# The x tiles of an attention and FP4 feed-forward layer loaded one by one, and the order of work on four engines written anew

## What is computed

```python
xn = layernorm(x)
q, k = l2norm(xn @ Wq.T), l2norm(xn @ Wk.T)      # 16 heads of 16
v = xn @ Wv.T
attn = softmax(q @ k.T + alibi, keys in a window of 128)   # ahead of and at the query
s = (attn @ v) @ Wo.T
h = silu(fq(xn) @ fq(w_gate).T) * (fq(xn) @ fq(w_up).T)    # 256 -> 704
g = silu(fq(h) @ fq(w_down).T)                             # 704 -> 256
out = x + s * g
# fq: FP4 (E2M1) rounding in blocks of 16 with a scale from the block's largest value
```

## Time and profile before

| | |
|---|---|
| median of three runs | 531.66 us (530.77 to 533.08) |
| the profiled execution | 533.7 us, of it a span of 532.0 us from the first to the last instruction |
| PE busy | 481.7 us, 91% |
| DVE, ACT, POOL busy | 427.3, 401.6, 428.6 us (80%, 75%, 81%) |
| mean granted TensorE clock | 0.962 |
| DMA | 29.36 MB, mean 55 GB/s |

### The profile page before, as it was taken

One profiled execution on the slowest core, in us unless ns is written; L12 is line 12 of the kernel. 1 busy time (PEld: TensorE's weight loads), 2 busy tenths in 40 slices (PEclk: granted clock), 3 DMA queues, 4 the chain that ended last, 5 costly groups with the idle time before them and its releaser, 6 DMA issues.

```text
span 532.0 us, 13894 instructions
## 1 busy us (share of the span) xinstructions
PE 481.7 (91%) x4962; PEld 410.7 (77%) x4962; DVE 427.3 (80%) x848; ACT 401.6 (75%) x572; POOL 428.6 (81%) x941
## 2 busy tenths in 40 slices
...
GB/s 308 59 40 41 40 41 42 41 52 52 51 90 51 52 51 76 28 51 41 51 90 52 52 51 89 52 22 41 51 41 52 51 51 51 51 51 51 14 10 31
DMA packets 78037, 29.36 MB, mean 55 GB/s; under 512 B 67472, under 2 KB 77456, under 8 KB 77968
## 3 DMA queue, kind: packets, MB, share of 16 engines
...
...
## 4 chain that ended last, share of the span: by engine, by line
PE 71%; DMA 8%; DVE 7%; POOL 6%; issue 5%; ACT 2%; POOLq 0%; ACTq 0%; DVEq 0%
PE up L277 12%; PE bank_b L468 11%; PE gt L430 11%; PE gt L277 9%; DMA qk_slots<-qk_stack 7%; PE bank_q L277 7%; PE scores L392 6%; PE gt L283 6%; PE bank_b L283 4%; PE bank_b L277 3%; PE gt L445 3%; DVE h_amax L602 1%; DVE qk_stack L661 1%; DVE hT_lo L641 1%; DMA keyfac<-key_factors 1%
## 5 line engine op out<-in xcount | busy, mean ns | idle before, releaser
L966 ACT ACTIVATE probs<-scores 128x1024 f32<-128x1024 f32 (+1 forms) x128 | 128.6, 1005 | 1.6 <-PE scores L392 0.8
L1101 POOL TENSOR_SCALAR_AFFINE_SELECT probs<-probs 128x512 f32<-128x512 f32 x128 | 82.5, 647 | 5.2 <-ACT probs L966 2.8
L1108 POOL TENSOR_SCALAR_AFFINE_SELECT probs<-probs 128x512 f32<-128x512 f32 x120 | 75.1, 638 | 2.0
L1134 POOL TENSOR_TENSOR h_q<-h_grid,h_scale 128x704 f32<-128x704 bf16 x32 | 44.4, 1388 | 38.2 <-DVE h_grid L624 38.2
L974 ACT ACTIVATE gate<-gt 128x704 f32<-128x704 f32 x32 | 24.3, 758 | 54.5 <-PE gt L277 54.5
L430 PE MATMUL gt<-wdn_hi,hT_hi 128*128 128x256 f32 x192 | 61.0, 318 | 0.6 <-DVE hT_lo L632 0.6
L468 PE MATMUL bank_b<-probs,vals 128*32 128x128 f32 x1984 | 60.8, 274 | 0.7 <-DVE att L686 0.7
L468 PEld LDWEIGHTS bank_b<-probs,vals 128*32 128x32 f32 x1984 | 52.2, 110 | 7.3 <-issue 7.2
L430 PE MATMUL gt<-wdn_lo,hT_hi 128*128 128x256 f32 x192 | 54.9, 286 | 0.0
L430 PE MATMUL gt<-wdn_hi,hT_lo 128*128 128x256 f32 x192 | 54.8, 285 | 0.0
L392 PE MATMUL scores<-qk_slots 48*128 48x256 f16 x480 | 47.2, 275 | 6.7 <-DMA qk_slots<-qk_stack 3.7
...
## 6 DMA issues: line engine op xcount, KB each, us to landing
...
qk_slots<-qk_stack SPq DMA_TRANSPOSE x32, 3.7
...
```

Source lines behind the costliest of these rows:

```text
L966: e.activation(probs[j % P_BUFS][:, grp, :, side(j), :], sc[:, :, :, side(j), :].rearrange("p b e h q -> p (b e) h q"), ACT.Exp).then_inc( ...
L1101: e.affine_select(out=own, in_=own, compare_op=ALU.is_ge, fill=0.0, base=0, pattern=[[0, GRP], [-1, P]], channel_multiplier=1).then_inc(s_ ...
L1108: e.affine_select(out=part, in_=part, compare_op=ALU.is_gt, fill=0.0, base=0, pattern=[[0, GRP], [1, P]], channel_multiplier=-1).then_inc( ...
L1134: e.tensor_tensor(blocks(h_q[t % 2][:, 0:FF]), blocks(h_grid[:]), per_block(h_scale[:]), ALU.mult).then_inc(s_q_h, 1)
```

## The change

Three things are altered. The last 16 tiles of x are no longer loaded in groups of four behind a store; each is loaded alone (128 KB) by a new `refill(t - 5)`, which SP issues right behind the transpose of tile t, for t from 5 to 20. It waits for `add_x` of the tile whose slot it fills. Second, on PE, DVE, ACT and POOL the first three turns and what follows the last full turn are written out call by call, in an order of their own. Third, the order within the repeated turn is new: on PE only the last two pieces change places (`wo_mm` before the end of `down_mm`), and on DVE, ACT and POOL several steps move. Two waits are added on PE: `up_mm` waits for `lo_x` (and the first for all rounded gate and up weights), `tr_tail` waits for `q_h`. What each function computes stays as it was.

The diff, with the indentation cut by twelve columns and the removed lines of the old loops left out:

```diff
@@ -37,7 +37,6 @@
 X_GROUP = 4
 X_RING = 16
 P_BUFS, Q_SLOTS, S_BUFS, V_SLOTS, Y_BUFS, FG_BUFS, XN_BUFS = 3, 3, 2, 4, 3, 2, 4
-X_LOADS = TILES // X_GROUP
 GRP = 4
 LAST = TILES - 1
@@ -157,7 +156,8 @@
 l_wproj, l_wg, l_wu, l_wd, l_wo, l_keyfac, l_ident, l_qkT = (
 sem(f"l_{n}") for n in ("wproj", "wg", "wu", "wd", "wo", "keyfac", "ident", "qkT"))
-l_x = [sem(f"l_x{i}") for i in range(X_LOADS)]
+l_x = [sem(f"l_x{i}") for i in range(X_RING // X_GROUP)]
+l_refill = [sem(f"l_refill{i}") for i in range(TILES - X_RING)]
 stored = [sem(f"stored{i}") for i in range(Y_BUFS)]
 s_lot = [sem(f"lot{i}") for i in range(len(GU_LOTS) + len(WD_LOTS))]
 s_scales = [sem(f"scales{i}") for i in range(WD_SCALES + 1)]
@@ -365,6 +365,9 @@
     product(gt_all[:, 512:512 + HALF], xT[t % 2], KT, wgu, HALF, FF).then_inc(s_gate_mm, 1)
 def up_mm(f):
+    if f == 0:
+        e.wait_ge(s_lo_wgu, len(WGU_GROUPS))
+    e.wait_ge(s_lo_x, f + LAG + 1)
     if f >= 1:
         e.wait_ge(s_hc, chain(f - 1, GRID))
     product(up_all[:, H0:512], xT[f % 2], KT, wgu, FF, FF + HALF)
@@ -403,6 +406,7 @@
 def tr_tail(g):
     if exists(g):
+        e.wait_ge(s_q_h, g + 1)
         e.wait_ge(s_pv_t, g + 1)
         e.wait_ge(s_pad_h, min(g + 1, 2))
         done = transposes(bank_b[:, 0:2 * P], [h_q[g % 2][:, k * P:(k + 1) * P] for k in range(4, FT)])
@@ -475,66 +479,93 @@
     transposes(bank_b, [pv_t[:, g, :] for g in range(4)]).then_inc(s_back, 1)
 tr_x(0)
-for t in range(END + 1):
-    f, g = t - LAG, t - LAG - 1
-    if exists(t - 2):
-        scores(t - 2, 3)
+qk_mm(0)
+v_mm(0)
+tr_x(1)
+qk_mm(1)
+tr_x(2)
+scores(0, 0)
+tr_wgu(0)
+v_mm(1)
+tr_wgu(1)
+scores(0, 1)
+tr_wgu(2)
+tr_wgu(3)
+tr_wgu(4)
+scores(0, 2)
+qk_mm(2)
+tr_wgu(5)
+v_mm(2)
+up_mm(0)
+gate_mm(0)
+up_mm_last(0)
+scores(0, 3)
+tr_x(3)
+tr_wd(0)
+tr_wd(1)
+scores(1, 0)
+tr_wd(2)
+scores(1, 1)
+scores(1, 2)
+scores(1, 3)
+for t in range(3, TILES):
+    qk_mm(t)
+    v_mm(t)
+    gate_mm(t - 2)
+    scores(t - 1, 0)
+    pv(t - 3)
+    tr_x(t + 1)
+    up_mm(t - 2)
+    tr_h(t - 3)
+    scores(t - 1, 1)
+    up_mm_last(t - 2)
+    tr_tail(t - 3)
+    scores(t - 1, 2)
+    down_mm(t - 3, 0, 4)
+    scores(t - 1, 3)
+    back(t - 3)
     if exists(t - 4):
...
+        wo_mm(t - 4)
+    down_mm(t - 3, 4, FT)
+gate_mm(TILES - 2)
+pv(TILES - 3)
+scores(TILES - 1, 0)
+up_mm(TILES - 2)
+up_mm_last(TILES - 2)
+tr_x(TILES + 1)
+tr_h(TILES - 3)
+scores(TILES - 1, 1)
+tr_tail(TILES - 3)
+scores(TILES - 1, 2)
+down_mm(TILES - 3, 0, 4)
+scores(TILES - 1, 3)
+down_mm(TILES - 3, 4, FT)
+back(TILES - 3)
+wo_mm(TILES - 4)
+up_mm(TILES - 1)
+gate_mm(TILES - 1)
+up_mm_last(TILES - 1)
+tr_h(TILES - 2)
+pv(TILES - 2)
+tr_tail(TILES - 2)
+down_mm(TILES - 2, 0, 4)
+back(TILES - 2)
+down_mm(TILES - 2, 4, FT)
+pv(TILES - 1)
+wo_mm(TILES - 3)
+tr_tail(TILES - 1)
+tr_h(TILES - 1)
+back(TILES - 1)
+wo_mm(TILES - 2)
+tr_tail(TILES)
+down_mm(TILES - 1, 0, 4)
+down_mm(TILES - 1, 4, FT)
+wo_mm(TILES - 1)
 def vector_program(e):
 def ln_stats(t):
-    e.wait_ge(l_x[t // X_GROUP], 16)
+    e.wait_ge(l_x[t // X_GROUP] if t < X_RING else l_refill[t - X_RING], 16)
     if t >= 1:
         e.wait_ge(s_moments, t)
     e.bn_stats(stats[:], x_all[:, t % X_RING, :]).then_inc(s_stats, 1)
@@ -766,103 +797,142 @@
 ln_moments(0)
 ln_stats(1)
 ln_moments(1)
-ln_stats(2)
 scales_w(0)
 amax_x(0)
 norm_w(0)
+ln_stats(2)
+lo_wproj(0)
+ln_moments(2)
+lo_wproj(1)
+lo_x(0)
 wide_x(0)
-lo_wproj(0)
-lo_x(0)
-lo_wproj(1)
 scales_w(1)
+squares(0)
+round_w(0)
+rscale_x(0)
+norm_x(0)
+lo_x(1)
+values(0)
+norm_w(2)
+ln_stats(3)
+up_x(0)
 scales_w(2)
...
+ln_moments(3)
+unit(0)
+amax_x(1)
+grid_x(0)
+wide_x(1)
+lo_qk(0)
+round_w(2)
+rscale_x(1)
+norm_w(4)
+squares(1)
+ln_stats(4)
+scales_w(WD_SCALES)
+round_w(4)
+norm_x(1)
+lo_wgu(0)
+norm_w(6)
+ln_moments(4)
+amax_x(2)
+lo_wgu(1)
+ln_stats(5)
+lo_wgu(2)
+unit(1)
+lo_wgu(3)
+up_x(1)
+lo_x(2)
+lo_qk(1)
+values(1)
+lo_wgu(4)
+grid_x(1)
+wide_x(2)
+lo_wgu(5)
+squares(2)
+values(2)
+rscale_x(2)
+round_w(6)
+hidden(0)
+norm_x(2)
+ln_moments(5)
+amax_h(0)
+lo_wd(0)
+lo_wo()
+up_x(2)
+lo_wd(1)
+unit(2)
+grid_x(2)
+lo_qk(2)
+lo_x(3)
+amax_x(3)
+wide_h(0)
+lo_wd(2)
+for t in range(3, TILES):
+    wide_x(t)
+    rscale_h(t - 3)
+    rscale_x(t)
+    norm_h(t - 3)
+    norm_x(t)
+    values(t)
+    up_h(t - 3)
+    grid_h(t - 3)
+    up_x(t)
+    if exists(t + 1):
+        amax_x(t + 1)
+    squares(t)
     if exists(t + 3):
         ln_stats(t + 3)
-    if exists(t + 1):
-        amax_x(t + 1)
-    if exists(t):
-        up_x(t)
-        grid_x(t)
+    lo_x(t + 1)
     if exists(t + 3):
         ln_moments(t + 3)
...
+    grid_x(t)
+    lo_h(t - 3)
+    hidden(t - 2)
+    unit(t)
+    lo_tail(t - 3)
+    amax_h(t - 2)
+    lo_qk(t)
+    denom(t - 3)
+    wide_h(t - 2)
+    if exists(t - 4):
+        gated(t - 4)
+    attend(t - 3)
+rscale_h(TILES - 3)
+norm_h(TILES - 3)
+up_h(TILES - 3)
+grid_h(TILES - 3)
+hidden(TILES - 2)
+lo_x(TILES + 1)
+amax_h(TILES - 2)
+lo_h(TILES - 3)
+wide_h(TILES - 2)
+rscale_h(TILES - 2)
+norm_h(TILES - 2)
+lo_tail(TILES - 3)
+up_h(TILES - 2)
+grid_h(TILES - 2)
+gated(TILES - 4)
+denom(TILES - 3)
+attend(TILES - 3)
+hidden(TILES - 1)
+amax_h(TILES - 1)
+wide_h(TILES - 1)
+lo_h(TILES - 2)
+rscale_h(TILES - 1)
+norm_h(TILES - 1)
+lo_tail(TILES - 2)
+up_h(TILES - 1)
+denom(TILES - 2)
+attend(TILES - 2)
+grid_h(TILES - 1)
+gated(TILES - 3)
+lo_tail(TILES - 1)
+lo_h(TILES - 1)
+denom(TILES - 1)
+attend(TILES - 1)
+gated(TILES - 2)
+lo_tail(TILES)
+gated(TILES - 1)
 def scalar_program(e):
@@ -989,71 +1059,94 @@
 e.dma_start(keyfac[:], keyfac_d).then_inc(l_keyfac, 16)
 hi_wproj(0)
 hi_wproj(1)
+square_w(0)
 hi_x(0)
-square_w(0)
 square(0)
+hi_x(1)
+hi_wo()
 square_w(1)
+square_x(0)
+hi_q(0)
+hi_k(0)
+square_w(2)
 square_w(3)
-square_w(2)
-hi_x(1)
-square_x(0)
+square(1)
 square_w(4)
+exp(0, 0)
 square_w(5)
 hi_wgu(0)
...
+exp(0, 1)
+hi_wgu(1)
+square_x(1)
+hi_wgu(2)
+hi_wgu(3)
+square_w(7)
+hi_q(1)
+hi_x(2)
+hi_k(1)
+exp(0, 2)
+square_w(6)
+hi_wgu(4)
+square(2)
+hi_wgu(5)
+silu(0)
+exp(0, 3)
+hi_wd(0)
+hi_x(3)
+hi_wd(1)
+exp(1, 0)
+square_x(2)
+exp(1, 1)
+hi_wd(2)
+hi_q(2)
+hi_k(2)
+exp(1, 2)
+exp(1, 3)
+square(3)
+square_h(0)
+square_x(3)
+silu(1)
+exp(2, 0)
+hi_x(4)
+keep_pv(0)
+hi_h(0)
+exp(2, 1)
+hi_tail(0)
+exp(2, 2)
+hi_q(3)
+hi_k(3)
+for t in range(3, TILES):
+    exp(t - 1, 3)
+    down_silu(t - 3)
+    square_h(t - 2)
     if exists(t + 1):
+        square_x(t + 1)
         square(t + 1)
...
+    silu(t - 1)
+    exp(t, 0)
+    hi_x(t + 2)
+    keep_pv(t - 2)
+    hi_h(t - 2)
+    exp(t, 1)
+    hi_tail(t - 2)
+    exp(t, 2)
     if exists(t + 1):
         hi_q(t + 1)
-    if t == 0:
-        hi_wgu(4)
-    if exists(t + 1):
         hi_k(t + 1)
-    if t == 1:
-        hi_wd(2)
-    if exists(t):
-        exp(t, 3)
+square_h(TILES - 2)
+exp(TILES - 1, 3)
+down_silu(TILES - 3)
+silu(TILES - 1)
+hi_h(TILES - 2)
+keep_pv(TILES - 2)
+hi_tail(TILES - 2)
+square_h(TILES - 1)
+down_silu(TILES - 2)
+keep_pv(TILES - 1)
+hi_tail(TILES - 1)
+hi_h(TILES - 1)
+hi_tail(TILES)
+down_silu(TILES - 1)
 def gpsimd_program(e):
@@ -1194,70 +1287,103 @@
     e.tensor_scalar(xn[t % XN_BUFS][:], x_all[:, t % X_RING, :], neg_mean[:], rsq[0][:, NS - 1:NS],
                     ALU.add, ALU.mult).then_inc(s_xn, 1)
-for i in range(S_BUFS):
-    pad_stack(i)
+pad_stack(0)
+pad_stack(1)
 pad_vals()
-for i in range(len(wdn)):
-    pad_wd(i)
-for slot in range(V_SLOTS):
-    ones(slot)
+pad_wd(0)
+pad_wd(1)
+ones(0)
 ln_parts(0)
 root(-2)
 x_norm(0)
 ln_parts(1)
 root(-1)
+norm_w(1)
+x_norm(1)
+norm_w(3)
+ln_parts(2)
+floor_ss(0)
 scale_x(0)
...
+ones(1)
+root(0)
+ones(2)
+round_w(1)
+q_x(0)
+x_norm(2)
+round_w(3)
+scale_x(1)
+ln_parts(3)
+floor_ss(1)
+norm_w(5)
+mask_own(0, 0)
+norm_w(7)
+root(1)
+ones(3)
+round_w(5)
+round_w(7)
+x_norm(3)
+q_x(1)
+floor_ss(2)
+ln_parts(4)
+root(2)
+mask_own(0, 1)
+scale_x(2)
+mask_own(0, 2)
+mask_own(0, 3)
+mask_own(1, 0)
+mask_prev(1, 0)
+mask_own(1, 1)
+mask_own(1, 2)
+mask_prev(1, 1)
+x_norm(4)
+q_x(2)
+mask_prev(1, 2)
+mask_own(1, 3)
+mask_prev(1, 3)
+ln_parts(5)
+scale_x(3)
+scale_h(0)
+pad_h(0)
+pad_h(1)
+for t in range(3, TILES):
+    q_h(t - 3)
+    floor_ss(t)
+    root(t)
+    mask_own(t - 1, 0)
+    mask_own(t - 1, 1)
+    mask_own(t - 1, 2)
     if exists(t + 2):
...
+        x_norm(t + 2)
+    mask_prev(t - 1, 0)
+    mask_prev(t - 1, 1)
+    mask_own(t - 1, 3)
+    mask_prev(t - 1, 2)
+    q_x(t)
+    if exists(t + 1):
+        scale_x(t + 1)
+    scale_h(t - 2)
+    mask_prev(t - 1, 3)
+    if exists(t - 4):
+        add_x(t - 4)
+    if exists(t + 3):
+        ln_parts(t + 3)
+q_h(TILES - 3)
+scale_h(TILES - 2)
+mask_own(TILES - 1, 0)
+mask_prev(TILES - 1, 0)
+mask_own(TILES - 1, 1)
+mask_own(TILES - 1, 2)
+mask_prev(TILES - 1, 1)
+mask_prev(TILES - 1, 2)
+mask_own(TILES - 1, 3)
+q_h(TILES - 2)
+mask_prev(TILES - 1, 3)
+scale_h(TILES - 1)
+q_h(TILES - 1)
+add_x(TILES - 4)
+add_x(TILES - 3)
+add_x(TILES - 2)
+add_x(TILES - 1)
 def sync_program(e):
@@ -1271,9 +1397,12 @@
```

(92 more changed lines are left out.)

134 lines of the change are left out of this document (removed).

## The result

| | before | after | ratio (95% interval) |
|---|---|---|---|
| median, first comparison | 531.21 us | 525.4 us | 0.9881 (0.9843 to 0.9918) |
| median, beside the first experiments | 531.65 us | 524.99 us | 0.9877 (0.985 to 0.9904) |
| range of the executions there | 529.4 to 532.9 | 524.0 to 525.5 | |

I read it with the cuts of the earlier trace rows: up to turn 4, turns 4 to 30, and the rest (stretch, length, PE, PEld, DVE, ACT, POOL, PEclk, DMA).

A forecast was written before the change was run, and what follows sets the result against it. PE was taken to bound turns 4 to 30 (busy 390.4 of 395.5 us), not start or end. Loop -1.3, start +1.7, end -4.7 sum to -4.3: 529.4 us for the profiled execution, 527.4 median; 8-in-10 range 520.5 to 534.5.

The forecast's parts named there:

- The repeated turn: Turns 4 to 30: PE's 14.48 us per turn stays the floor, and no result comes late in the new order.
- the first rival: Repeated turn: POOL ends root late, so every turn pays; at 0.3 us in 27 turns 535.5 us; chance 0.16.
- The late transposes: DMA transposes in the loop: seven stay late, each with an instruction packet; three to eleven possible, 0.7 us each.
- The term of the loop: Turns 4 to 30: 1.3 us gained, 0.3 in each of two windows and 0.1 in each of seven.
- The start: Up to qk_mm(3): 1.7 us lost, bounds 0.5 to 3.0, with qk_mm(3) at 65.2 instead of 63.48.
- (a): Start, DVE's queue up to the end of round_w(4): ends at 38.9 us, 1.4 earlier without blocked durations.
- (b): Start: tr_wgu(1) waits for round_w(4), at 38.9 instead of 31.91; lo_qk(1) ends at 47.7 instead of 45.87.
- (c): Start, from qk_mm(2) to the end of gate: gate ends at 55.6 us against 52.6, where silu starts.
- (d): Start, ACT's chain from silu to scores: 9.6 us and 0.3 of gaps, qk_mm(3) at 65.5.
- The end: Last long chain and final projections: 4.7 us gained, bounds 1.5 and 6.0.
- The clock: End: PE's clock stays full instead of 0.53 for 7.3 us, as PE's idle stretch gets work; 2.2 us gained.
- The third rival: Nothing to see: clock falls in the end as now (+2.2), start costs its upper bound (+1.3): 530.9 us; chance 0.18.

The follow-up runs named there:

- loop_only: Kernel before with turns 3 to 31 in the new order and two added PE waits; start, end and grouped x loads old: 529.53 us, ratio 0.9971.
- x_only: Kernel before with tiles 16 to 31 of x loaded singly and two added PE waits, every engine's order old: 529.06 us, ratio 0.9965.
- tail_only: Kernel before with only what follows the last full turn in the new order, two added PE waits, grouped x loads: 525.38 us, ratio 0.9894.
- round_first: Changed kernel with DVE's round_w(4) moved ahead of the scales of the last weight lot: 525.18 us, ratio 0.9892.
- pool_light: Changed kernel with POOL's four weight roundings cut to 16 columns, queues and waits the same: 524.28 us, ratio 0.989.
- chain_late: Changed kernel with five PE pieces at the end (up and gate of tile 31, tr_h(30), pv(30)) in the old order: 528.0 us, ratio 0.9938.
- filler: Kernel before with useless projections of tile 31 added on PE behind pv(31), where it idles ahead of tr_h(31): 529.36 us, ratio 0.9957.

## Why the prediction was right, point by point

**The repeated turn.** The floor of 14.48 us stayed, and the turn laid out by hand agrees with the trace within 0.2 us but for `root`, 0.4 earlier than thought, and POOL's last mask, which ends 3.3 into the next turn and not 3.0. So the first rival (`root` late, every turn pays) did not occur: `unit` starts 10.83 into the turn, right behind `hidden`, not behind `root`.

**The late transposes** stayed, six for seven, each with a packet of queue 8, as said. The term of the loop was 1.3 us, against 3.0 in the profiles and 1.5 by `loop_only` (interval 0.6 to 2.5). The step that was sized too small was to give the load of x ahead of a transpose 0.3 us in two turns only. `x_only` gained 1.9 us (1.0 to 2.7) in the old order, an unknown part of it by where its packets fell: where load and packet met in `tail_only`, the scores waited 1.1 and 1.5 us, and the two stalls of the same kind in before were priced at 0.3 of load each from a single trace. I also did not see that the new turn by itself moves store and load over 9 us ahead of the transpose, though `add_x` and `store` stood in the diff; the cause named (single loads behind the transpose) is therefore the second of two sufficient ones, and the new loads bring nothing on top. That the term lies near the 1.5 measured is in part luck. That the refill behind the transpose costs 0 was right: 16 of them, and the transposes beside them land in the median 3.7 us.

**The start** was priced at +1.7 with bounds 0.5 and 3.0; it measured +0.5 alone and 0.4 on the mark `qk_mm(3)` in after's trace; against the other traces with the old start the mark of after is 0.2 to 1.0 later. Link by link: (a) `round_w(4)` ended at 37.1 instead of 38.9, since `scales_w(2)` was not blocked (1.4; POOL's `round_w(1)` began at 24.29, when DVE's two small steps of 23.61 to 24.06 were done) and the scales of the last lot took 2.8 us and not 3.7; the price of a blocked instruction fell on `x_wide` instead, 1.23 for 0.17. (b) `lo_qk(1)` ended at 46.2 instead of 47.7, early by what (a) was. (c) the first silu 54.22 instead of 55.6. (d) ACT's chain 9.64 for 9.9. So the chain was right in kind from link (c) on. But `round_first` shows that link (b) was no bound: with `tr_wgu(1)` 2.7 us earlier nothing moved. Links of PE, DVE, ACT and POOL lie level there, and `pool_light` shows that POOL's is not the longest. Which work has to shrink to shorten the start stays open.

**DVE and GpSimd.** `x_wide` on 16 columns took 1.23 us beside POOL's large `round_w(1)` (it ended at 26.98, the step of POOL that ran beside it at 26.95), and 0.17 when that was cut. The Trainium skill ("SBUF — State Buffer", Who interferes with whom) says that a DVE instruction in a two-port mode and a GpSimd one lock each other out for its whole length; `pool_light` agrees with its 0.17. By that rule the forecast made the start 65.5, without it 64.1; the mark was 63.86. The forecast took the rule at the wrong instruction: which one is hit depends on what is beside it in the new queues.

**The end** was priced at 4.7 with bounds 1.5 and 6.0, and measured 5.4 in the profiles, 5.6 by `tail_only`. The two terms were right one by one. `q_h` 2.2 earlier: 2.12 (it ends 43.56 us behind `qk_mm(31)` before, 41.44 after), and `chain_late` gives back 2.7. The clock 2.2: `filler` measures 2.3. Together 4.4 of 5.4; of the 1.0 us that is left 0.8 lies behind `q_h`, where PE waits 1.25 us for DVE's and POOL's steps, in `filler` 2.2. `hidden(31)` came 32.50 us into the stretch, forecast 32.6.

**The sum** came out 2 us short of the gain. By the single parts the start was 1.2 too dear, the end 0.9 and the loop 0.2 too small, all in the same direction. Each lies within its bounds, the start right at its lower one. The third rival (clock falls, start at its bound) failed on the clock.
